# One 1 MB transfer per weight slot in blocks 1 to 3, instead of two of 512 KB

## What is computed

```python
xn  = layernorm(x)
out = x + mamba2(xn) + moe_lora_ffn(xn)

# mamba2: proj = xn @ in_proj_w.T -> gate (4096), conv input (4096 + 2*1024), dt (64)
#   causal 4-tap convolution + silu, dt = softplus(dt + bias), dA = exp(dt * A)
#   state = state * dA + (dt * x) outer B ;  y = state . C + x * D   (a scan over tokens)
#   y = group_rmsnorm(y) * norm_weight * silu(gate) ;  return y @ out_proj_w.T
# ffn: xn @ W_base.T + b_base + 2 * sum over the top 2 of 8 experts of the rank-16 LoRA terms
```

## Time and profile before

| | us |
|---|---|
| median of 3 runs | 3392.07 |
| lowest, highest | 3388.98, 3392.81 |
| the profiled execution | 3389.2 |
| its span in the trace | 3387.5 |
| granted TensorE clock, mean | 0.994 of full |
| TensorE (PE) busy | 3315.3, 98% |
| VectorE (DVE) busy | 2475.2, 73% |
| weight loads from `w_split` | 732 of 512 KB, median 3.5 from issue to landing |

### The profile page before, as it was taken

How to read it: one execution, slowest core, us unless ns; L and a number is a source line. 1 busy time by engine, 2 the same in 40 slices (tenths; PEclk the granted TensorE clock), 3 DMA queues, 4 the chain that set the end, 5 groups by cost and what they waited for, 6 DMA issues and landing times.

```text
span 3387.5 us, 53697 instructions
## 1 busy us (share of the span) xinstructions
PE 3315.3 (98%) x16224; PEld 2767.0 (82%) x16224; DVE 2475.2 (73%) x3865; ACT 1522.0 (45%) x3454; POOL 1154.6 (34%) x1079
## 2 busy tenths in 40 slices
PE   7999999999999999999999999999999999999999
PEld 5787777887888888888878888888878888888887
DVE  6898898997677777777558766777755877766773
ACT  3565555554354444444225444444422544444441
POOL 3554554554223333323203332332320332333231
PEclk9899999999999999999999999999999999999999
DMA  6667676676665555555466555555547555555554
GB/s 221 234 249 258 237 250 223 240 251 251 234 214 178 185 170 187 176 179 185 159 206 211 181 181 174 187 174 181 192 156 245 168 185 174 176 186 174 181 173 156
DMA packets 183949, 672.80 MB, mean 199 GB/s; under 512 B 20864, under 2 KB 22016, under 8 KB 183168
## 3 DMA queue, kind: packets, MB, share of 16 engines
q1 hardware_dynamic: 161280, 584.91, 51.5%
q10 hardware_dynamic: 22400, 84.42, 7.1%
HBM read 532.41 MB, written 136.84 MB: 198 GB/s over the span
## 4 chain that ended last, share of the span: by engine, by line
PE 82%; DVE 10%; issue 3%; ACT 2%; DMA 1%; POOL 1%; ACTq 0%; DVEq 0%; SPq 0%; POOLq 0%
PE dense L843 23%; PE dense L845 22%; PE dense L844 22%; PE pY L927 6%; DVE conv_us L1172 3%; PE pD L947 1%; PE pX L911 1%; DMA w_hl<-w_split 1%; PE dense L880 1%; DVE xT L1180 1%; DVE w_hl L1078 1%; DVE E L1207 1%; PE pS L845 1%; PE pU L843 1%; PE pU L845 1%
## 5 line engine op out<-in xcount | busy, mean ns | idle before, releaser
L843 PE MATMUL dense<-xn_hi,w_hl 128*128 128x512 f32 x2880 | 1152.1, 400 | 29.9 <-issue 11.3
L845 PE MATMUL dense<-xn_hi,w_hl 128*128 128x512 f32 x2880 | 1127.8, 392 | 0.0
L844 PE MATMUL dense<-xn_lo,w_hl 128*128 128x512 f32 x2880 | 1126.0, 391 | 0.0
L843 PEld LDWEIGHTS dense<-xn_hi,w_hl 128*128 128x128 f32 x2880 | 544.1, 189 | 140.2 <-issue 23.0
L845 PEld LDWEIGHTS dense<-xn_hi,w_hl 128*128 128x128 f32 x2880 | 543.3, 189 | 116.8
L844 PEld LDWEIGHTS dense<-xn_lo,w_hl 128*128 128x128 f32 x2880 | 544.7, 189 | 114.2 <-issue 7.5
L1172 DVE SCALAR_TENSOR_TENSOR conv_us<-conv_in,const_g,conv_us 128x512 f32<-128x512 f32 x576 | 458.9, 797 | 13.6
L843 PE MATMUL dense<-z_hi,w_hl 128*128 128x512 f32 x1024 | 412.1, 402 | 2.9 <-DVE acc L1255 2.1
L461 POOL TENSOR_TENSOR rstd<-ssq,eps_t 128x1 f32<-128x1 f32 x128 | 40.1, 313 | 1099.7 <-ACT xD L654 1099.7
L845 PE MATMUL dense<-z_hi,w_hl 128*128 128x512 f32 x1024 | 401.4, 392 | 0.0
L437 POOL TENSOR_TENSOR xD<-x_ck,D_g 128x512 f32<-128x512 f32 x128 | 181.6, 1419 | 643.4 <-ACT x_ck L624 552.2
(11 more groups left out here) (175 smaller groups left out, 4920.5 us busy)
## 6 DMA issues: line engine op xcount, KB each, us to landing
w_hl<-w_split SPq DMA_DIRECT2D x732, 512.0 KB, 3.5
w_split<-w_hl SPq DMA_DIRECT2D x244, 512.0 KB, 3.3
cum_b<-cum_scratch ACTq DMA_DIRECT2D x128, 512.0 KB, 4.8
w_raw<-w_slots_dram SPq DMA_DIRECT2D x122, 512.0 KB, 5.1
acc<-x_tr_dram ACTq DMA_DIRECT2D x4, 2048.0 KB, 11.3
out_tr_dram<-acc ACTq DMA_DIRECT2D x16, 512.0 KB, 4.3
BC<-x_tok_dram SPq DMA_DIRECT2D x6, 512.0 KB, 4.6
conv_us<-x_tok_dram SPq DMA_DIRECT2D x6, 512.0 KB, 5.9
```

The lines of the kernel that those rows point to most:

```text
L843: nc.tensor.matmul(out, lhs[0], rhs[0], start=start, stop=False)
L844: nc.tensor.matmul(out, lhs[0], rhs[1], start=False, stop=False)
L845: return nc.tensor.matmul(out, lhs[1], rhs[0], start=False, stop=stop)
```

## The change

The two transfers that fill a slot in blocks 1 to 3 become one. The scratch tensor is laid out so that one slot is 8 KB in a row, and the stores of block 0 write their 4 KB halves into it. SyncE waits for the second half of a slot to be done and then issues one transfer of 1 MB. TensorE's semaphores become one per buffer; it waits on the same count before either half.

```diff
-        w_split = nc.dram_tensor("w_split", [2 * SLOTS, 128, 1024], F32).ap()
+        w_split = nc.dram_tensor("w_split", [SLOTS, 128, 2048], F32).ap()
-        w_loaded = [[sem(f"w_loaded{s}{h}") for h in range(2)] for s in range(2)]
+        w_loaded = [sem(f"w_loaded{s}") for s in range(2)]
+            def slot(s):
+                return w_hl[s][:].rearrange("p h a b -> p (h a b)").bitcast(F32)
...
-                            sp.dma_start(w_split[bass.ds(pair * 4 + (2 * s - 4), 1)].rearrange("o p f -> (o p) f"),
+                            sp.dma_start(w_split[bass.ds(pair * 2 + (s - 2), 1), :, 0:1024].rearrange("o p f -> (o p) f"),
                                          half(s, 0)).then_inc(w_stored[s][0], 16)
...
                     with sp.Fori(first, end) as pair:
                         for s in range(2):
-                            for h in range(2):
-                                sp.wait_ge(dense_done, q * (2 * SLOTS) + pair * 4 + (2 * s + h + 1))
-                                sp.dma_start(half(s, h),
-                                             w_split[bass.ds(pair * 4 + (2 * s + h), 1)].rearrange("o p f -> (o p) f"))\
-                                  .then_inc(w_loaded[s][h], 16)
+                            sp.wait_ge(dense_done, q * (2 * SLOTS) + pair * 4 + (2 * s + 2))
+                            sp.dma_start(slot(s), w_split[bass.ds(pair * 2 + s, 1)].rearrange("o p f -> (o p) f"))\
+                              .then_inc(w_loaded[s], 16)
...
                     for s in range(2):
-                        for h in range(2):
-                            if first_block:
+                        if first_block:
+                            for h in range(2):
                                 sp.wait_ge(w_stored[s][h], (SLOTS // 2) * 16)
-                            sp.wait_ge(dense_done, (q + 1) * (2 * SLOTS) + (2 * s + h + 1))
-                            sp.dma_start(half(s, h), w_split[2 * s + h]).then_inc(w_loaded[s][h], 16)
+                        sp.wait_ge(dense_done, (q + 1) * (2 * SLOTS) + (2 * s + 2))
+                        sp.dma_start(slot(s), w_split[s]).then_inc(w_loaded[s], 16)
...
-                        pe.wait_ge(w_loaded[k % 2][h], load_n(q, g, k) * 16)
+                        pe.wait_ge(w_loaded[k % 2], load_n(q, g, k) * 16)
```

More of the change, by code:

```diff
@@ L306, in split_pairs @@
                             sp.wait_ge(lo0_done, pair * 2 + (s - 1))
-                            sp.dma_start(w_split[bass.ds(pair * 4 + (2 * s - 4), 1)].rearrange("o p f -> (o p) f"),
+                            sp.dma_start(w_split[bass.ds(pair * 2 + (s - 2), 1), :, 0:1024].rearrange("o p f -> (o p) f"),
                                          half(s, 0)).then_inc(w_stored[s][0], 16)
                             sp.wait_ge(lo1_done, pair * 2 + (s - 1))
-                            sp.dma_start(w_split[bass.ds(pair * 4 + (2 * s - 3), 1)].rearrange("o p f -> (o p) f"),
+                            sp.dma_start(w_split[bass.ds(pair * 2 + (s - 2), 1), :, 1024:2048].rearrange("o p f -> (o p) f"),
                                          half(s, 1)).then_inc(w_stored[s][1], 16)
```

## The result

The changed kernel takes 3417.86 us (median of 4 runs, 3415.81 to 3421.25), the kernel before 3391.31 beside it (4 runs, 3388.98 to 3392.81). The ratio is 1.008, with a 95% interval of 1.0062 to 1.0097: slower, by 26.5 us. The direction was as forecast and the time is inside the range, but the loss is 1.5 times the 18.2 us of the sum.

A forecast was written before the change was run, and what follows sets the result against it. TensorE, busy for 98% of the span, was taken as the bound. Slots 8 and 9 3 x (1.7 + 2.2), old waits -2.5, output stores +2.2, clock falls +6.8: +18.2 us, median 3410 us, range 3397 to 3430.

The follow-up runs named there:

- late_two: The kernel before, but in blocks 1 to 3 both 512 KB transfers of a slot wait until the whole slot has been used: 3406.53 us, ratio 1.0059.

## What to carry to other kernels

Merging two prefetches into one costs the lead of the first (here a shortest window of 7.8 us became 5.1): count the shortest time from the release of the buffer to its use, and compare it with the landing of the merged transfer beside everything else that is then in flight, block by block. Here 318 of 366 merged transfers cost some 3 us (0.1%) when they stood alone, and the other 48 alone cost 33, more than the 26.5 of all, so look for the few places where other queues burst, and leave those alone. On a kernel that keeps TensorE at 98%, price each new wait with the clock that it may cost; here that came to more than a third of the loss.

## What I had not expected of the hardware

- Which idle moments lower the clock can't be read from their length. It stayed at 1.00 behind 2.26 us at slot 9 of block 1, and fell behind these, where TensorE was busy for 2.48 of 3.5 us (idle for 0.51 us twice behind VectorE):

```profile
1024.00:1027.50 3.50, 2.48 (x20) 2.19 (x20) 3.46 (x6) 1.90 (x4) 1.38 (x1) 1.00 0.68 219
1027.50:1030.90 3.40, 3.40 (x12) 2.72 (x10) 3.29 (x6) 1.90 (x3) 0.00 (x0) 0.50 0.58 242
```

  The kernel before works through the same place 4 us earlier, with idle moments of 0.53 and 0.50 us and no fall. A delay at one place can thus bring a clock fall at another.
- Transfers on ScalarE's queue changed with the order of the weight loads and not with their size: cum_b lands in 3.7 us in the median instead of 4.8, while output stores, which are issued 0.6 to 1.0 us behind a weight load, went from 4.3 to 6.3. late_two, with twice as many loads of half the size, has the same 3.7 and 6.3. Why a store waits so long behind one slot's load was not tried.
